# Mixing tiles of 25 tokens instead of 24, and the last batch's query drain reordered

## What is computed

```
q = layernorm(x) ; k = v = ctx
qh, kh, vh = Wq q, Wk k, Wv v          # 8 heads of 64
qh = softmax(qh, over the 64 of a head) / 8 ;  kh = softmax(kh, over the 2048 columns)
context = kh vh^T  (64 x 64 per head) ;  out = Wo (context^T qh) + bo
x = x + out / |out| * g * sqrt(256)    # norm over the 256 channels, per column

h = layernorm(x) ; hn = h * rsqrt(mean(h^2))          # per token
res, pre, post = three small projections of hn, 16 + 4 + 4 numbers per token
H = sinkhorn(res / 0.1), 50 rounds of row and column normalisation of a 4 x 4 matrix
H = (1 - s) I + s H ;  s = sigmoid(gate)
y = (sum over streams of softmax(pre) * stream) W_branch
x = x + (H applied to the four streams) + softmax(post)_i * y in stream i
```

## Time and profile before

| | us |
|---|---|
| median of 3 runs | 2565.55 |
| lowest, highest | 2563.75, 2566.59 |
| the profiled execution | 2568.32 |
| its span in the trace | 2566.6 |

### The profile page before, as it was taken

One profiled execution on the slowest core, in us unless ns is written; L12 is line 12 of the kernel. 1 busy time (PEld: TensorE's weight loads), 2 busy tenths in 40 slices (PEclk: granted clock), 3 DMA queues, 4 the chain that ended last, 5 costly groups with the idle time before them and its releaser, 6 DMA issues.

```text
span 2566.6 us, 35379 instructions
## 1 busy us (share of the span) xinstructions
PE 2413.9 (94%) x12004; PEld 1914.3 (75%) x12004; DVE 1726.8 (67%) x4114; ACT 1172.8 (46%) x2464; POOL 1094.4 (43%) x1107
## 2 busy tenths in 40 slices
PE   7999999999999999999999999999999999899774
PEld 6888878887878778787877778777778876777521
DVE  4454567676767557776776567667687756877786
ACT  4454444545354444545444454544445344453333
POOL 1635536172635427262543616245272633623410
PEclk9999999999999999999999999999999999999887
DMA  7112221313122432312213243343302233231376
GB/s 237 50 66 99 74 92 56 108 41 103 63 70 96 128 119 83 113 62 70 95 67 99 80 153 93 120 141 101 123 34 90 92 114 117 76 117 44 88 221 193
DMA packets 200145, 255.72 MB, mean 100 GB/s; under 512 B 43550, under 2 KB 109854, under 8 KB 199966
## 3 DMA queue, kind: packets, MB, share of 16 engines
q1 hardware_dynamic: 199966, 253.47, 31.3%
HBM read 177.53 MB, written 75.89 MB: 99 GB/s over the span
## 4 chain that ended last, share of the span: by engine, by line
PE 57%; DVE 20%; POOL 11%; issue 8%; ACT 3%; SPq 1%; DMA 1%; DVEq 0%; POOLq 0%; ACTq 0%
PE kc_bank L642 15%; PE big L701 7%; PE tb L743 4%; PE tb L757 3%; PE tb L628 3%; PE big L616 3%; PE big L618 3%; PE big L617 3%; POOL x_tr L1535 3%; DVE stats L889 3%; PE big L675 3%; PE big L677 2%; PE big L676 2%; PE tb L686 2%; POOL q_sb L1515 2%
## 5 line engine op out<-in xcount | busy, mean ns | idle before, releaser
L1254 ACT COPY turned<-tb 128x512 f32<-128x512 f32 x512 | 298.7, 587 | 755.3 <-PE tb L686 487.9
L701 PE MATMUL big<-merged,turned 128*128 128x256 f32 x2048 | 495.0, 385 | 36.3 <-ACT turned L1254 24.5
L642 PE MATMUL kc_bank<-ctxt,turned 128*128 128x256 f32 x2048 | 479.5, 380 | 3.0 <-DMA ctxt<-in_ctx_t 3.0
L701 PEld LDWEIGHTS big<-merged,turned 128*128 128x128 f32 x2048 | 385.8, 191 | 110.7 <-ACT turned L1254 19.4
L642 PEld LDWEIGHTS kc_bank<-ctxt,turned 128*128 128x128 f32 x2048 | 374.6, 191 | 54.6 <-issue 8.9
L1490 POOL TENSOR_TENSOR in_l<-x_sb,in_h 128x512 fp32r<-128x512 f32 x128 | 167.8, 1340 | 574.9 <-ACT in_h L1294 574.8
L1515 POOL TENSOR_TENSOR q_sb<-q_sb,qsum 128x1024 f32<-128x1024 f32 x128 | 243.8, 1904 | 274.4 <-DVE qsum L971 274.4
L980 DVE SCALAR_TENSOR_TENSOR on<-big,nrm,g_rows 128x256 f32<-128x256 f32 x256 | 111.9, 479 | 220.7 <-POOL nrm L1528 220.4
L616 PE MATMUL big<-in_h,wk_h 128*128 128x512 f32 x512 | 237.7, 464 | 15.4 <-DVE in_l L821 10.0
L675 PE MATMUL big<-wq_h,in_h 128*128 128x512 f32 x512 | 236.4, 462 | 10.9 <-DVE q_sb L959 10.4
L757 PE MATMUL tb<-mix_ld,mix_w 121*96 121x512 f32 (+2 forms) x324 | 187.9, 677 | 57.7 <-POOL mix_w L1497 28.0
(11 more groups left out here) (149 smaller groups left out, 4308.5 us busy)
## 6 DMA issues: line engine op xcount, KB each, us to landing
mix_ld<-streams SPq DMA_DIRECT2D x157, 240.0 KB
ctxt<-in_ctx_t SPq DMA_DIRECT2D x64, 512.0 KB, 4.0
x_sb<-in_x SPq DMA_DIRECT2D x64, 512.0 KB, 6.1
x_tr<-in_x_t SPq DMA_DIRECT2D x64, 512.0 KB, 6.6
streams<-x_sb SPq DMA_DIRECT2D x64, 512.0 KB, 3.1
stage<-in_ctx SPq DMA_DIRECT2D x60, 512.0 KB, 4.1
out<-mix_out SPq DMA_DIRECT2D x157, 192.0 KB, 2.2
streams<-y_sb SPq DMA_DIRECT2D x32, 256.0 KB, 2.0
```

Of the source, the lines that this page charges most:

```text
L642: t = nc.tensor.matmul(kc_bank[:, 0:C], turned[n % 3][:, j * P:(j + 1) * P], ctxt[:, nt, :], start=nt == 0, stop=nt == NT - 1)
L701: t = nc.tensor.matmul(big[2 + p % 2][:, half], turned[n % 3][:, dt * P:(dt + 1) * P], merged[:, dt, :], start=dt == 0, stop=dt == DT - 1)
L1254: nc.scalar.copy(turned[k % 3][:], tb[n % 2][:]).then_inc(s_tba, 1)
```

## The change

The mixing tile has 25 tokens, not 24. For the last queries (batch 15), group 3's iteration steps are spread over places up to query step 11 instead of 18, so its coefficients are stored at step 12 instead of 19, and no mix is placed in query steps 14 to 26. In steps 16 to 19 of that batch `query_transpose(i - 4)` stands before `attention_out(i - 5)` instead of behind it. Nothing is computed differently.

```diff
--- before.py
+++ after.py
@@ -56,7 +56,7 @@
     FG = DT * NQ + NT
     QB = 3
 
-    TOK = 24
+    TOK = 25
     PARTS = STREAMS + 1
     ONES = TOK * PARTS
     MIX_TILES = [[(FIRST[n] * C + at, min(TOK, size * C - at)) for at in range(0, size * C, TOK)]
@@ -126,7 +126,8 @@
     starts = [order_of_places.index(keys_of(FIRST[gr] + GROUPS[gr])[4]) for gr in range(LAST)] + [len(order_of_places)]
     ready = []
     for gr in range(LAST):
-        free = [place for place in order_of_places[starts[gr]:starts[gr + 1] - 8]
+
+        free = [place for place in order_of_places[starts[gr]:starts[gr + 1] - (8 if gr < LAST - 1 else STEPS - 12)]
                 if place[0] == "Q" and 5 <= place[2] < NT + 4 or place[0] == "B" and (place[2] >= 2 or place[2:] > (1, 1))
                 or place[0] == "A" and place[2] >= 2 and place[3]]
         free = free[:SINK]
@@ -160,7 +161,7 @@
             known += ready.pop(0)[1]
             put_loads(place)
             since = min(since, PACE - 6)
-        if place[0] != "Q" and place[2] == 0:
+        if place[0] != "Q" and place[2] == 0 or place[:2] == ("Q", NB - 1) and place[2] >= NT - 2:
             continue
         since += 1
         if mixed < loaded and since >= PACE:
@@ -799,11 +800,14 @@
                         key_transpose(b, DT - 1, NQ - 1)
                     if i < 2:
                         key_context(b, DT - 1, 2 * i + 1)
+                    first = b == NB - 1 and i >= NT
+                    if 4 <= i < NT + 4 and first:
+                        query_transpose(b, i - 4)
                     if 5 <= i < NT + 5:
                         attention_out(b, i - 5)
                     if 10 <= i < NT and i % 2 == 0:
                         return_pair(b, (i - 10) // 2)
-                    if 4 <= i < NT + 4:
+                    if 4 <= i < NT + 4 and not first:
                         query_transpose(b, i - 4)
                     if b + 1 < NB and i in (17, 19, 21, 23):
                         key_logits(b + 1, 0, (17, 19, 21, 23).index(i))
```

## The result

| | before | after |
|---|---|---|
| median, us | 2565.55 | 2608.18 |
| lowest to highest, 5 runs each | 2563.34 to 2566.59 | 2605.39 to 2608.45 |
| span of the profiled execution | 2566.6 | 2605.0 |

The ratio is 1.0165, with a 95% interval of 1.015 to 1.018. The kernel became 42.6 us slower; the prediction had 61 (2627, range 2588 to 2678).

A forecast was written before the change was run, and what follows sets the result against it. It took TensorE to bound most slices, and VectorE's iteration and mixing, with DMA engines 0.87 busy, the tail. Terms summed to -13.7 without transfers and +75 for them, +61: 2627 us as median, range 2588 to 2678.

The forecast's parts named there:

- The deal: Mixing tiles' DMAs: rows go in equal shares to the largest divisor up to 16 engines; busiest get 35 per tile, not 14.
- The price of a row: Mixing transfers: a row of 2,048 bytes costs one engine 0.10 us (0.085 to 0.116).
- the forecast for the tail: Stretch before the last batch's own outputs: 165 us in place of 101, +64 (+39 to +90).
- Own outputs: Last batch's own outputs at the end: about 48 us against 38.6, +9 (+4 to +17).
- Middle batches: Batches before the end: three mixes fewer, -3; big loads late behind mixing transfers, +2 (-1 to +10).
- Steps 11 to 15 and the drain: Batch 15's last queries without iteration and mixing: -5.4 in steps 11 to 15, -8.3 in the drain.
- the order: Batch 15, steps 16 to 19: transposes ahead of outputs, -1 (-2.6 to +2).
- The steps that move: Thirteen iteration steps earlier: six in query steps at 0.43 us, seven in key places at 0.2; +4 (+3 to +6).
- 1 (2552): Mixing transfers: rows dealt evenly over 16 engines, leaving only -13.7, so 2552; 6 in 100.
- 2 (2571): Tail: loads and stores overlap within an engine or start on different engines; tail about 120 us, total 2571; 7 in 100.
- 3 (2675 and up): Tail: ScalarE's copy waits for late stores and queues run dry; tail 200 to 215 us, total 2675 to 2690; 12 in 100.
- 4, that the drain gives nothing: Drain: the last pair's chain stays as long, so -13.7 becomes about -4, total 2637; 15 in 100.

The follow-up runs named there:

- store cut: Changed kernel with only each 100-row store issued as 96 + 4 rows, loads of 125 rows whole: 2596.62 us (kernel before on that chip 2568.1).
- load cut: Changed kernel with only each 125-row load issued as 120 + 5 rows, stores of 100 rows whole: 2569.05 us (kernel before on that chip 2568.1).
- both cut: Changed kernel with each 125-row load issued as 120 + 5 rows and each 100-row store as 96 + 4: 2568.39 us, ratio 1.0009.
- the bad deal: Kernel before, tiles of 24 tokens, with each 120-row load issued as 115 + 5 rows: 2594.51 us, ratio 1.0112.

## Why the prediction was right, point by point

**The deal.** Shown, in both directions and in three sizes. Equal shares on the largest divisor up to 16, loads and stores adding on the same engines:

| kernel | rows on the busiest engines | pace, us | us per row |
|---|---|---|---|
| whole change; tiles of 25 alone | 25 + 10 = 35 | 2.97 | 0.085 |
| store cut | 25 + 7 = 32 | 2.73 | 0.085 |
| kernel before, load cut 115 + 5 | 24 + 6 = 30 | 2.47 | 0.082 |
| load cut | 9 + 10 = 19 | 2.28 | not the bound |
| both cut | 9 + 7 = 16 | 2.19 | not the bound |

The coefficients' small rows lie beside these (25 of 16 bytes on each of five engines with 125 rows); no run varied them, and the price per row includes them. The one tile of 8 tokens in the trace of before was enough to see it. The Trainium skill (DMA: Bandwidth & Descriptors, section "Why a DMA increments its semaphore by 16 and not by 1") has the rule with the lowest-numbered engines taken first. No view here numbers the engines, but that 10 rows of a 100-row store add to 25 of a load at the full price is what that rule makes of them.

**The price of a row: the term that was mis-sized.** I took 0.10 us between 0.085 and 0.116; it was 0.085. The tail's 1,647 rows make 140 us at that price (measured 144.6) and 165 at mine. The step that was off is how I got the two dearer prices. I took the DMA share times 16 engines over the throughput. That is the mean time of one row's packet, not the pace of an engine, and the share of 1.08 had said that packets overlap. In the changed kernel both can be read from one stretch: the same formula gives 0.47 x 16 x 2,048 / 162,000 = 0.095 us for a packet, while the busiest engines take 0.085 us for each row. The row to take was the cheapest one, the spill at 387 GB/s. At that price the forecast for the tail is +39 in place of +64; measured +41.9.

**Own outputs.** Forecast +9, measured +6 (43.1 for 37.1). The same price gives 418 x 0.085 + 4.5 = 40, so some 3 us are left; I put them down to landing times, which no run took apart.

**Middle batches.** Forecast -3 for three mixes and +2 for late loads. From batch 0's first maximum to batch 14's, the five kernels with tiles of 25 take 2072.7 to 2075.4 us, seven of those with 24 take 2077.7 to 2080.5, and the one with the bad deal in tiles of 24 takes 2075.0. The missing mixes are there: batches 7 and 12 have key places shorter by 1.0 and 2.0 us in all five. The rest of the spread is the query steps that take one of two times, seen above. Late loads show in no stretch: the other key places up to batch 13's agree within 0.2 us in all thirteen kernels. Under a mix every 12 us the bad deal costs nothing that can be seen.

**Steps 11 to 15 and the drain.** Forecast -5.4 and -8.3 with -1 for the order: measured -6.2 and -7.4 (-6.9 with tiles of 24). The size of the whole was right, its parts were not: that they add up was luck. The order gives 1.8 to 3.9 us, not 1. The wait that I had feared behind the early transposes is there when the iteration stays (TensorE waits 4.24 us for GpSimd), and it pays anyway:

```profile
2393.47 1.11 PE L687 MATMUL tb<-ident,q_sb 128*128 128x128 f32 x4 [4.24 <-POOL q_sb L1519]
2394.38 2.98 PE L702 MATMUL big<-merged,turned 128*128 128x256 f32 x8
```

**The steps that move: the term that failed.** Forecast +4 (3 to 6), measured +9 with tiles of 24 (batch 14's queries +2.4, key places +5.3, steps 5 to 11 +1.4) and +10.8 in the whole change. The 1.7 us between them go with TensorE's clock: the profiled execution of the whole change has 0.98 in batch 15's key places, and TensorE 66.78 us busy for 65.09, with the same waits:

```profile
2251.60:2325.30 73.70, 66.78 (x294) 48.59 (x293) 57.51 (x164) 38.52 (x82) 12.75 (x17) 0.98 0.32 100
```

The kernel with the store cut has the same (73.5 us at 0.98), those with the load cut and with both cut do not (72.0 at 1.00); why, no run shows. The six query steps cost 3.8 us, 0.6 each and not 0.43. For key places I had "TensorE is the bound; I take 0.2 each". Four of the seven steps land in batch 14's key places and cost nothing that can be told; three land in batch 15's, where 5.3 us are lost. What waits there is TensorE, for the merged context in front of everything else, and the price hangs on what lies before it on VectorE, not on a mean per step. Which of the steps do it is open, as said above.

**The mixes away.** I counted their places in the tail but not their price: in the kernel before they give 0.3 us where they were and cost 1.8 in the tail.

**Rivals.** 1 (2552) and 2 (2571) fall with the pace of 2.97 and with the store cut. 3 (2675 and up) falls: ScalarE does wait 92.2 us for stores, but the pace is what 35 rows give at the spill's price, with no gaps on top. 4, that the drain gives nothing, was meant as a drain that isn't shorter; the drain is shorter by 7 us and the sum over the kernel is nevertheless 0.9996. Its number was right for another reason. In all, -13.7 + 75 was forecast. The spans have about -10 (start to batch 14 -6.7, moved steps +10.8, steps 11 to 15 and drain -13.6) and +48; of the -10 some 3.6 are what differs between executions before batch 14, and the medians give +42.6. That the total fell well inside the range comes from the range of the row's price, whose low end, +39, was the right one.

**Slips that changed nothing.** The earlier trace rows has 35 slices at 9, not 37. Rival 2's terms add up to some 2574 and not 2571, rival 3's to 2668 to 2683.

## What to carry to other kernels

Before a tile size is changed, factor the rows of its DMAs: 120 and 96 rows use 15 and 16 engines, 125 and 100 use 5 and 10, and 4% more per tile made a tile take 45% longer where transfers became the bound (2.97 for 2.05 us) and cost nothing that can be seen where they aren't. Look in the trace for the odd last tile of a loop: here it gave the deal away before anything ran. And take an engine's price from a stretch that its rows fill, not from packet times.

When dependent work is moved earlier under another engine's bound, ask what waits behind it at each new place, not what a step costs on average; the gain at the old place (9 us) and the loss at the new one (9 us) were both real. Take the edits apart even when the sum is zero: the order of the transposes was worth 3.9 us of the drain with the iteration left in place, and 1.8 with it moved.

## What the runs showed of the hardware beyond this

Five busy DMA engines move a row of 2,048 bytes in 0.082 to 0.085 us each, 24 to 25 GB/s for an engine, with loads and stores on the same engines and others partly idle. The 16 engines of the spill have the same pace over 1 us (387 GB/s / 16 = 24.2), and 20 us of loads on all of them are a little slower (365 / 16 = 22.8).

A short VectorE sum that takes 0.18 us elsewhere (first row, the same form) took 1.16 us beside a GpSimd operation on 128 x 512 elements (two of them in the POOL row):

```profile
2304.01 0.18 DVE L1071 TENSOR_TENSOR sku<-sku,skr 128x32 f32<-128x32 f32 x1
...
2304.80 2.49 POOL L1494 TENSOR_TENSOR in_l<-x_sb,in_h 128x512 fp32r<-128x512 f32 x2 [2.62 <-ACT in_h L1298]
2304.95 1.16 DVE L1074 TENSOR_TENSOR skv<-skv,skr 128x32 f32<-128x32 f32 x1 [0.76 <-ACT skr L1345]
```

It isn't a single case. All executions of that line in the changed kernel:

```profile
L1074 DVE TENSOR_TENSOR skv<-skv,skr x25: 162/191/1569, 415.2 to 2557.0; 128x32 f32<-128x32 f32 x15, 128x16 f32<-128x16 f32 x10
```

Seven of the 25 take 0.64 to 1.57 us. Each of the seven starts while a GpSimd operation runs and ends 0.03 to 0.05 us after that operation does, as if it had to wait for it. The traces of before show the same in six of 25. No run moved the GpSimd operations, so this is an order in time and not a tried cause. Such instructions are among the long ones in batch 15's key places and may be part of the 5 us that the moved steps cost there.
